# Second edge stage: the three layers of the path-weight network, spread over both groups of an octet and taken from three successive octets

## The reference, cut to what matters

```python
r = jax.nn.silu(edge_rbf @ M1)      # 64000 x 16 @ 16 x 64
r = jax.nn.silu(r @ M2)             # 64 x 64
r = jax.nn.silu(r @ M3)             # 64 x 64
tpw = (r @ M4).reshape(-1, 4, C)    # path weights, C = 64
...
x0 = up0[snd]
x1 = up1[snd]
...
m0e = tpw[:, 0] * x0 * sh0[:, None] + tpw[:, 3] * jnp.einsum('ecx,ex->ec', x1, sh1) * inv3
m1e = tpw[:, 1][:, :, None] * x0[:, :, None] * sh1[:, None, :] + tpw[:, 2][:, :, None] * x1 * sh0[:, None, None]
msg0 = jax.ops.segment_sum(m0e, rcv, num_segments=n)
msg1 = jax.ops.segment_sum(m1e, rcv, num_segments=n)
```

## Time and profile before

| | us |
|---|---|
| median of 3 runs (lowest, highest) | 1760.73 (1758.09, 1762.08) |
| profiled execution, its own time | 1765.67 |
| its span, first to last instruction | 1763.9 |
| PE busy | 1350.7 (77%) |
| DVE busy | 935.0 (53%) |
| ACT busy | 616.5 (35%) |
| POOL busy | 957.8 (54%) |
| mean granted clock of PE, share of full | 0.868 |

### The profile page before, as it was taken

How to read it: one execution, slowest core, us unless ns; L and a number is a source line. 1 busy time by engine, 2 the same in 40 slices (tenths; PEclk the granted TensorE clock), 3 DMA queues, 4 the chain that set the end, 5 groups by cost and what they waited for, 6 DMA issues and landing times.

```text
span 1763.9 us, 39415 instructions
## 1 busy us (share of the span) xinstructions
PE 1350.7 (77%) x13431; PEld 801.7 (45%) x13431; DVE 935.0 (53%) x2353; ACT 616.5 (35%) x1897; POOL 957.8 (54%) x1008
## 2 busy tenths in 40 slices
PE   3668778877788775657778787888887878856999
PEld 1345454554455444343444444444444444543458
DVE  4445555454433343655555555555555556676763
ACT  2233333333333332243343433334343433323420
POOL 0677777777777774016665666666566656500000
PEclk9699988988988898778888888888888888977999
DMA  6333333333333330323333333333333333300001
GB/s 199 96 81 75 81 81 75 76 86 75 87 75 82 75 85 20 134 69 100 92 102 89 101 89 93 91 96 93 94 91 89 97 90 103 85 24 1 1 10 38
DMA packets 78954, 141.94 MB, mean 80 GB/s; under 512 B 25483, under 2 KB 34091, under 8 KB 78249
## 3 DMA queue, kind: packets, MB, share of 16 engines
q0 software_dynamic: 40128, 81.99, 17.8%
q1 hardware_dynamic: 38632, 57.46, 10.9%
HBM read 134.69 MB, written 4.67 MB: 79 GB/s over the span
## 4 chain that ended last, share of the span: by engine, by line
PE 44%; POOL 16%; issue 15%; DVE 12%; ACT 5%; DMA 5%; DVEq 2%; SPq 1%; ACTq 0%; POOLq 0%; PEldq 0%
POOL ring L412 16%; PE ps L932 8%; PE ps L946 8%; DVE arena L1357 5%; PE ps L919 5%; DMA ring<-mtab,src 4%; PE ps L968 4%; PE ps L1093 3%; PE ps L1084 3%; PE ps L762 2%; DVE arena L1355 2%; ACT wfT L583 1%; PE ps L694 1%; DVE arena L1347 1%; PE ps L775 1%
## 5 line engine op out<-in xcount | busy, mean ns | idle before, releaser
L422 POOL DMA_INDIRECT arena<-utab,src x500 | 473.3, 947 | 368.9 <-issue 143.5
L412 POOL DMA_INDIRECT ring<-mtab,src x500 | 482.3, 965 | 205.7 <-issue 197.2
L1223 DVE TENSOR_TENSOR arena<-ps,ring 128x1024 f32<-128x1024 f32 x125 | 153.0, 1224 | 290.7 <-PE ps L762 278.2
L932 PE MATMUL ps<-arena 64*128 64x256 f32 x1016 | 171.6, 464 | 144.7 <-DVE arena L1357 100.8
L571 ACT ACTIVATE arena<-ps 128x512 f32<-128x512 f32 x193 | 116.8, 605 | 360.0 <-PE ps L919 358.2
L1357 DVE TENSOR_TENSOR arena<-ps,arena 128x768 f32<-128x768 f32 x252 | 228.3, 948 | 0.0
L932 PEld LDWEIGHTS ps<-arena 64*128 64x128 f32 x1016 | 102.2, 216 | 184.1 <-DVE arena L1357 66.9
L946 PE MATMUL ps<-arena 128*8 128x256 f32 x4032 | 184.1, 330 | 0.0
L1347 DVE TENSOR_TENSOR arena<-arena,ps 128x16 f32 x512 | 87.3, 171 | 174.1 <-PE ps L955 116.8
L762 PE MATMUL ps<-arena,ring 128*64 128x128 f32 x2000 | 162.1, 313 | 0.0
L753 PE MATMUL ps<-ring 128*32 128x97 f32 x1000 | 49.3, 270 | 138.8 <-DMA ring<-mtab,src 136.4
(11 more groups left out here) (222 smaller groups left out, 1864.4 us busy)
## 6 DMA issues: line engine op xcount, KB each, us to landing
arena<-in_eaT SPq DMA_DIRECT2D x125, 256.0 KB
ring<-mtab,src POOLq DMA_INDIRECT x500
arena<-utab,src POOLq DMA_INDIRECT x500
arena<-in_rbf SPq DMA_DIRECT2D x132, 32.0 KB
ring<-in_fw SPq DMA_DIRECT2D x2, 1024.0 KB, 5.8
utab<-arena SPq DMA_DIRECT2D x1, 2048.0 KB, 7.5
XT<-in_xT SPq DMA_DIRECT2D x2, 1000.0 KB
arena<-in_x SPq DMA_DIRECT2D x1, 1920.0 KB, 9.5
```

The lines of the kernel that those rows point to most:

```text
L412: pool.indirect_dma_start(MR[:, n % 4, k, 0:H], None, mtab, bass.IndirectOffsetOnAxis(ap=src[:, 4 * n + k:4 * n + k + 1], axis=0)).then_in ...
L422: pool.indirect_dma_start(G1[:, n % NSLOT, k, :], None, utab, bass.IndirectOffsetOnAxis(ap=src[:, 4 * n + k:4 * n + k + 1], axis=0)).then_ ...
L932: mm = pe.matmul(ps[:, 2 + h, a * D:(a + 1) * D], R3[hs, c:c + P], m4[hs, :], start=True, stop=True)
L1223: dve.tensor_tensor(RM[:, n % 2, :, :, :], ps[:, 1, 0:P].rearrange("p (t q) -> p t q", t=4).unsqueeze(3).broadcast_to([P, 4, KH, WIN]), SW ...
```

## The change

Three things, all in the order of PE's and ACT's work in the second edge stage:

- Per octet o, PE now does: weights(n+1), **layer 2 of octet o+1**, segment(n), mix1(n), turn(n-1), weights(n+2), **layer 1 of octet o+2**, segment(n+1), mix1(n+1), **layer 0 of octet o+3**, turn(n). One layer in the even half and two in the odd half, where there were two and one.
- ACT now does: silu of layer 2 (o+1), collect(n), mix1(n), silu of layer 1 (o+2), collect(n+1), silu of layer 0 (o+3), mix1(n+1).
- Ahead of the loop six layers are computed instead of four: all three of octet 0, layers 0 and 1 of octet 1, and layer 0 of octet 2. Counts of `s_mlp` and `s_silu` follow a running number `at` instead of 3 x octet + layer. There are two layers more in all.

No operation changes its shape; POOL's and SP's instructions are the same.

```diff
-MLPS = 3 * NO + 4
+MLPS = 3 * NO + 6
...
-            def silu(j, o, layer_):
-
-                act.wait_ge(S["s_mlp"], j * MLPS + 3 * o + layer_ + 10)
+            def silu(j, at, layer_):
+
+                act.wait_ge(S["s_mlp"], j * MLPS + at + 10)
...
-                for layer_ in range(3):
-                    silu(j, 0, layer_)
-                silu(j, 1, 0)
+                for at, layer_ in enumerate((0, 1, 2, 0, 1, 0)):
+                    silu(j, at, layer_)
                 for o in range(NO):
-                    silu(j, o + 1, 1)
+                    silu(j, 3 * o + 6, 2)
                     collect(j, 2 * o, 0)
                     mix1(j, 2 * o)
-                    silu(j, o + 1, 2)
-                    silu(j, o + 2, 0)
+                    silu(j, 3 * o + 7, 1)
                     collect(j, 2 * o + 1, 1)
+                    silu(j, 3 * o + 8, 0)
                     mix1(j, 2 * o + 1)
...
-            def layer(j, o, layer_, par=0, rbn=0, after=True):
+            def layer(j, at, o, layer_):
 
                 if layer_ == 0:
-                    pe.wait_ge(rbl[par], (j * RBS + rbn + 1) * 32)
-                    w, x, k = m1, RBF[:, par, :], 16
+                    pe.wait_ge(rbl[o % 3], (j * RBS + o // 3 + 1) * 32)
+                    w, x, k = m1, RBF[:, o % 3, :], 16
                 else:
                     w, x, k = ((m2, R1, H), (m3, R2, H))[layer_ - 1]
-                if after:
-                    pe.wait_ge(S["s_silu"], j * MLPS + 3 * o + layer_)
+                if at:
+                    pe.wait_ge(S["s_silu"], j * MLPS + at)
...
                 if octet is not None:
-                    pe.wait_ge(S["s_silu"], j * MLPS + 3 * octet + 3)
+                    pe.wait_ge(S["s_silu"], j * MLPS + (3 * octet + 4 if octet else 3))
...
-                for layer_ in range(3):
-                    layer(j, 0, layer_, after=layer_ > 0)
-                layer(j, 1, 0, 1)
+                for at, (o, layer_) in enumerate(((0, 0), (0, 1), (0, 2), (1, 0), (1, 1), (2, 0))):
+                    layer(j, at, o, layer_)
                 weights(j, 0, 0, 0)
                 for o in range(NO):
                     n = 2 * o
                     weights(j, n + 1, 1, None)
-                    layer(j, o + 1, 1)
+                    layer(j, 3 * o + 6, o + 1, 2)
                     segment(j, n, 0, 2 * (o % 3))
                     mix1(j, n)
-                    layer(j, o + 1, 2)
                     turn(j, n - 1, 1)
                     weights(j, n + 2, 0, o + 1)
-                    layer(j, o + 2, 0, (o + 2) % 3, (o + 2) // 3)
+                    layer(j, 3 * o + 7, o + 2, 1)
                     segment(j, n + 1, 1, 2 * (o % 3) + 1)
                     mix1(j, n + 1)
+                    layer(j, 3 * o + 8, o + 3, 0)
                     turn(j, n, 0)
```

## The result

The changed kernel takes **1717.12 us** (median of 4 runs, 1713.42 to 1718.51), the kernel before 1759.64 us beside it (4 runs, 1758.09 to 1762.08). The ratio is 0.9759, 95% interval 0.974 to 0.9777: 42.5 us less, where 37.3 were forecast (1723.4, range 1704 to 1747).

What follows compares the result with a forecast made beforehand. PE was taken to bound the stage. Eight cycles x 2.6 (20.8), plus clock 22.4, less 2.4 for new falls, plus tail 1, less 4.5 for start and end: 37.3 us off 1760.73 gives 1723.4, range 1704 to 1747.

Steps and rivals of the forecast that it cites:

- What bounds it: Second edge stage: PE sets the pace; its 138 us idle, almost all ahead of weights, or its clock can be won.
- The odd f=0 half: Half behind the even f=6 silu wait: without that wait, about 5.6 us at full clock, where it took 8.21 at 0.58.
- The 7 x 3.2 of the sum: Clock term: the low clock in odd f=0 halves goes, 3.2 us in each of seven cycles, 22.4 us.
- The first rival: Clock stays low: the fall belongs to the f=5 stop or new DVE waits draw one; 1743.4 us, chance 0.30.
- Even halves: Halves ending in weights(n+2): silu waits and one layer go, partly held by DVE's round; 6.95 us less a cycle.
- Odd halves: The other halves of a cycle: one layer more each, and a later square root at f=5; +4.4 us a cycle.
- the second rival: More: even halves shift the f=5 stops so less PE work meets low clock; one gone, 19 more, 1704; chance 0.07.
- Allowance for new falls: New PE waits of about 1.4 us for products at even f=3 and f=4 may lower the clock: 0.3 us a cycle.
- The added wait: Odd f=5: silu of layer 0 ahead of ACT's square root makes DVE's product and PE's weights 0.8 us later.
- Stops: PE's two long f=5 waits for DVE's products: even one grows from 4.41 to 5.0 us, odd one to 5.1.
- The slower rival: Both f=5 stops grow and each keeps the clock low one stretch more, 6.4 us a cycle; 1795 us, chance 0.08.
- Start and end: Fixed costs: two more layers ahead of the loop +3.9 us, one layer at the end +0.6, last 14 groups -1.

Runs made afterwards that it cites:

- The change without the spread: Changed kernel with two layers in the even half again, one in the odd, layer 2 still at the even half's head: 1717.36 us, ratio 0.9766.
- the spread without the lead: Changed kernel with layer 2 and its silu behind the attention step as before, one layer in even halves, two in odd: 1790.54 us, ratio 1.0172.
- the order of ACT alone: Kernel before, ACT's silu of layer 2 ahead of the attention step in all even groups except f=5, PE's order untouched: 1715.59 us, ratio 0.9737.
- The kernel before without the f=6 wait: Kernel before, ACT's silu of layer 2 ahead of the scaling in even groups with f=6 only: 1737.05 us, ratio 0.9866.
- with the stops gone: Kernel before with f=5 square roots moved ahead of the silu of layer 1 (even groups) or layer 0 (odd): 1655.66 us, ratio 0.941.
- the changed kernel with the wait put in: Changed kernel, ACT's silu of layer 2 put behind the copy and scaling in even groups with f=6 only: 1763.82 us, ratio 1.0023.
- the changed kernel with the early square root: Changed kernel, ACT's f=5 square root moved ahead of the silu of layer 2 (even groups) or layer 1 (odd): 1647.97 us, ratio 0.9366.

## Why the prediction was right, and which term was off

The mechanism was right, and the total was 5.2 us short.

- **What bounds it: right.** The idle time ahead of weights was what could be won. Until a silu: forecast near 0, measured 0 (42.8 before). Until products: forecast about 125, measured 121.7 (95.0 before).
- **The silu's lead over PE is the cause: shown.** The change without the spread has the whole gain (1717.4), the spread without the lead loses 30 us, and the order of ACT alone, which takes the same silu out from behind the attention step, gives the gain too (1715.6).
- **The odd f=0 half: right.** Forecast 5.6 us at full clock; 5.75 in the mean. The 7 x 3.2 of the sum stand in the trace of the kernel before: seven of its eight odd f=0 halves take 8.18 to 8.21 us at 0.58 and one 4.99 at 1.00, and within the one at 1096.18 the clock is 0.50 from 1097.50 to 1102.50. The kernel before without the f=6 wait has 4.99 there in all eight cycles. The first rival's condition, the fall as an after-effect of the stop, is out: the wait alone, taken away, ends the fall at that place, and with the stops gone there are falls behind waits of 1.75 still. The prediction held for that rival that the wait of the first cycle drew no fall. It didn't see that the fall of that cycle came behind the next wait, at even f=3.
- **Even halves**, forecast then measured mean: f=6 5.5, 5.84; f=1 4.5, 4.64; f=3 4.55, 4.59; f=4 4.5, 4.73; f=5 8.3, 8.32; f=2 5.2, 4.99; f=0 **6.0, 5.18**. At f=6 the cut of a layer (0.6) isn't there in full.
- **Odd halves:** f=1 4.8, 4.91; f=2 5.6, 5.73; f=3 4.5, 4.65; f=4 4.45, 4.69; f=5 9.0, 8.97; f=6 **7.0, 5.75**.
- **The mis-sized term** is those two halves, which follow the even f=5 stop. The sum has the clock stay low through odd f=6 ("+1.1 (low clock)") and into even f=0: 13.0 us, where seven of the eight pairs take 10.4 to 10.7. The row of 1111.06:1116.66 shows why: the clock is 0.65 in that half, and weights behind it take 1.14 us. In the kernel before, the same half had 0.50 and the next weights still took 1.92. So the low stretch behind this stop ended sooner; only in the first cycle is it as forecast (7.0). That is the second rival's condition, at one of the two stops: by the means 8 x 2.1, 17 us, where it had 19. The forecast wasn't further off because the other halves give about 10 of it back: most are 0.1 to 0.3 longer than forecast, since DVE's round is nearer 4.6 than 4.5. That these misses offset each other in part is luck. Why the stretch is shorter isn't settled. The length of the stop doesn't decide it: with the lead alone, two stops of 4.37 us in the same place are followed by next weights of 2.08 us (877.87) and of 1.13 (1195.03).
- **Allowance for new falls, -0.3 a cycle: not drawn.** The new waits for products are 1.28 to 1.54 us at even f=3 and f=4, as forecast (1.4), and no fall follows one. It was no idle fear: in the spread alone such a wait is 1.70 to 1.98 us and does draw one, each cycle, and with ACT's order alone one of 1.55 and one of 1.72 do.
- **The added wait: right.** Forecast 0.8 in odd f=5, measured 8.97 against 8.24, and gone when the silu stands behind. ACT, timeline of the changed kernel:

```profile
1144.28 0.39 ACT L578 ACTIVATE arena<-ps 128x256 f32<-128x256 f32 x1 [0.98 <-PE ps L945]
1144.56 0.59 ACT L571 ACTIVATE arena<-ps 128x512 f32<-128x512 f32 x1
1145.17 1.28 ACT L601 ACT_TABLE_LOAD   x1
```

  The table load is behind the silu, where it followed the copy in the earlier trace rows.
- **Stops:** forecast 5.0 and 5.1, measured 5.00 and 5.12. The slower rival (both keep the clock low for one stretch more) didn't come.
- **Start and end: right.** The first layer to the first weights is 10.71 us, 3.9 more than before as forecast; the end +0.6 as forecast; the groups behind the last stop +0.4, where 1 us less was forecast.
- **Cycle and clock:** 78.4 to 78.6 from the second cycle on (80.3 the first), forecast 79.7; stage 0.91, forecast 0.89. The forecast's low time, 28% of a cycle, takes the low clock as 0.50; the half at 1133.29 of the kernel before has that figure over its whole 5.93 us.
- **POOL and squares: right.** The three slots bridge the 4.5 us groups (4.59 to 4.73 us at f=3 and 4, where four gathers take 4.99 by the row of L422): no first product of DVE waits for a gather, its idle time is 44.0 us of issue and 33.6 until PE. And no half shows values that wait at f=2 (4.99 in the even ones).

What a prediction could have found, and this one didn't look for: that the silu could simply be moved on ACT, with no layer moved. And nothing in it said where the silu's table load goes when ACT's order changes: taking the f=6 wait out of the old order won 24 us, putting that silu back in the new one cost 47, since 1.28 us of table load came into the wait with it.

## What to carry to other kernels

When PE waits for a short eviction that stands behind a long one on ACT, try the order of ACT's queue before moving PE's work, and place it by the step: in the groups where another engine waits for the long step (here the square root), leave that first. Price a wait on PE with the low clock that may follow it, here up to 3.2 us for a wait of 1.75. See where the table load lands: it belongs in a place where nobody waits for ACT. Expect the low stretch to go over to the next wait of like size when one is removed, as in six of eight cycles here from the wait of 1.75 us to that of 1.74. Ask which engine comes next before summing up: the same silu waits were worth 42 us with two stops in the cycle and 7.7 once the gathers set the pace.

## What the runs showed of the hardware

- **Idle times of 1.55 to 1.75 us on PE were followed by a fall of the granted clock to 0.50 in some places and not in others.** Behind a wait of 1.75 the clock was 0.58 over a half that took 5.15 us at 1141.69, and 1.00 with the same wait at 1119.94 in the same execution; behind a wait of 1.74, 0.51 at 1106.62 and 0.50 at 1024.72 (the kernel before without the f=6 wait). In the kernel with ACT's order alone one followed a wait of 1.55 (943.97; 0.57 from 945 to 949) and none another wait of 1.55 (1025.92; 0.99 over the half behind it). In the changed kernel waits of 1.54 us and less were never followed by a fall, nor was the one of 1.65 at 1435.73. Which of two like waits draws the fall isn't settled by these runs; with 1.75 at two places and no stop near, it was one in each cycle.
- **The low stretch behind a stop isn't of one length, and the stop's length doesn't set it:** behind 4.41 us of idle time it covered the whole half and more (weights of 1.92 at 1139.22), behind 5.00 it ended within the half (1.14 at 1116.66) or ran through it (2.08 at 880.03), and behind 4.37 in one execution of the lead alone it did both (2.08 at 877.87, 1.13 at 1195.03).
- **Gathers came at one every 1.24 us where POOL hardly waited for a slot (5.5 of 521.45 us, the changed kernel with the early square root):** 394.8 busy and 122.5 in issue for 416 instructions, four of them 4.97 us a group, which is the cycle of 70.2 us over 14 groups (5.0) of that kernel.
- **The table load of 1.28 us ran as soon as ACT came to it, ahead of its activation's wait:** in the kernel before, the load at 1085.08 followed the square root (0.21 us from 1084.85) and ended 5.19 us before its silu started at 1091.55. Behind the scaling, in the changed kernel with the wait put in, it lay in PE's wait (1095.67, silu at 1096.96).
